# Third cross attention: keys split into F32R parts and replaced in place; both 16-head attentions: exponentials ahead of the chunk copies

## The reference, cut to what matters

```python
q = (x @ Wq).reshape(b, n, h, d).transpose(0, 2, 1, 3)
k = (context @ Wk).reshape(b, -1, h, d).transpose(0, 2, 1, 3)
v = (context @ Wv).reshape(b, -1, h, d).transpose(0, 2, 1, 3)
sim = jnp.einsum('bhid,bhjd->bhij', q, k) * d ** -0.5
attn = jax.nn.softmax(sim, axis=-1)
out = jnp.einsum('bhij,bhjd->bhid', attn, v)
return out.transpose(0, 2, 1, 3).reshape(b, n, h * d) @ Wo + bo
```

## Time and profile before

| | before |
|---|---|
| median of the runs | 2400.94 us |
| profiled execution, own time | 2401.57 us |
| its span | 2399.7 us |
| PE busy | 2227.5 us (93%) |
| DVE busy | 1857.3 us (77%) |
| ACT busy | 1493.9 us (62%) |
| POOL busy | 686.7 us (29%) |

### The profile page before, as it was taken

The page is one execution under the profiler, slowest core; times in us unless marked ns, Lnnn a source line. Parts: engine busy times, 40 slices in busy tenths (PEclk is TensorE's granted clock), DMA queues, the critical chain, the costliest instruction groups (busy, mean ns, idle before and its releaser), DMA issues.

```text
span 2399.7 us, 49297 instructions
## 1 busy us (share of the span) xinstructions
PE 2227.5 (93%) x14668; PEld 1913.3 (80%) x14669; DVE 1857.3 (77%) x4483; ACT 1493.9 (62%) x3090; POOL 686.7 (29%) x926
## 2 busy tenths in 40 slices
PE   7899999999899999995479999999998999989999
PEld 6788888888698788873257888888886788879998
DVE  3798888888876788887975887887888666866666
ACT  5566666666444677767886666666664655636666
POOL 2255555555412122210001111111102442422334
PEclk9999999999899999997589999999998999989999
DMA  8444454445201444430025445444442000114545
GB/s 216 118 141 129 142 146 142 131 138 147 69 0 37 125 132 126 138 111 16 0 67 152 135 134 152 138 145 140 140 132 62 1 1 2 38 54 141 140 140 158
DMA packets 461646, 256.58 MB, mean 107 GB/s; under 512 B 25664, under 2 KB 442332, under 8 KB 461532
## 3 DMA queue, kind: packets, MB, share of 16 engines
q1 hardware_dynamic: 461532, 255.27, 37.8%
HBM read 150.10 MB, written 105.12 MB: 106 GB/s over the span
## 4 chain that ended last, share of the span: by engine, by line
PE 75%; DVE 11%; ACT 6%; issue 5%; POOL 0%; ACTq 0%; DVEq 0%; POOLq 0%
PE ps_o L904 13%; PE ps_s L891 11%; PE ps_p L87 7%; PE ps_p L89 6%; PE ps_p L88 6%; PE ps_t L881 6%; PE ps_o L1474 3%; PE ps_t L1474 2%; PE ps_t L3129 2%; PE ps_s L3111 2%; PE ps_o L3129 2%; PE ps_s L87 2%; ACT a_keys L1022 2%; DVE a_sm L1197 2%; PE ps_s L89 2%
## 5 line engine op out<-in xcount | busy, mean ns | idle before, releaser
L904 PEld LDWEIGHTS ps_o<-a_val,a_pt 128*128 128x128 f32 (+2 forms) x3200 | 416.3, 193 | 34.9 <-issue 8.4
L904 PE MATMUL ps_o<-a_val,a_pt 128*128 128x128 f32 (+2 forms) x3200 | 426.6, 277 | 5.7 <-ACT a_pt L1059 3.6
L891 PE MATMUL ps_s<-a_keys,a_zt 128*128 128x308 f32 (+1 forms) x1024 | 414.3, 491 | 14.6 <-ACT a_keys L1022 9.8
L1031 ACT ACTIVATE a_stage<-ps_p 128x512 f32<-128x512 f32 (+1 forms) x370 | 221.2, 598 | 277.0 <-PE ps_p L89 275.5
L1197 DVE TENSOR_REDUCE a_sm<-a_e 128x16 f32<-128x1232 f32 (+1 forms) x192 | 234.3, 1220 | 179.4 <-ACT a_e L1067 178.9
L1059 ACT ACTIVATE a_pt<-ps_t 128x512 f32<-128x512 f32 (+1 forms) x448 | 225.1, 505 | 144.0 <-PE ps_t L881 142.7
L1022 ACT ACTIVATE a_keys<-ps_p 128x308 f32<-128x308 f32 x603 | 256.8, 427 | 79.5 <-PE ps_p L89 79.0
L87 PE MATMUL ps_p<-ct_hi,a_mt_hi 96*128 (+1 forms) x603 | 292.2, 485 | 0.0
L881 PE MATMUL ps_t<-ident,a_e 128*128 128x128 f32 (+1 forms) x1600 | 261.8, 276 | 25.1 <-POOL a_e L1214 13.6
L1067 ACT ACTIVATE a_e<-a_e 128x1232 f32<-128x1232 f32 (+1 forms) x192 | 203.9, 1062 | 52.8 <-DVE a_e L1189 36.4
L1214 POOL TENSOR_TENSOR a_e<-a_e,a_rs 128x539 f32<-128x539 f32 (+1 forms) x192 | 165.8, 891 | 231.3 <-DVE a_rs L1202 230.0
(11 more groups left out here) (437 smaller groups left out, 4939.4 us busy)
## 6 DMA issues: line engine op xcount, KB each, us to landing
a_vals<-a_stage SPq DMA_DIRECT2D x160, 512.0 KB, 3.5
a_val<-a_vals SPq DMA_DIRECT2D x128, 576.0 KB
f_w<-in_L_ffn_W_dram SPq DMA_DIRECT2D x129, 256.0 KB, 2.6
a_vals<-a_stage SPq DMA_DIRECT2D x40, 416.0 KB
a_val<-a_vals SPq DMA_DIRECT2D x64, 256.0 KB
a_val<-a_vals SPq DMA_DIRECT2D x128, 40.0 KB
x<-in_x_dram SPq DMA_DIRECT2D x8, 512.0 KB, 7.0
out_dram<-x SPq DMA_DIRECT2D x7, 512.0 KB, 6.7
```

Of the source, the lines that this page charges most:

```text
L891: eng.matmul(c.ps_s[:, b, 0:nh * KEYS], zt, keys[:, h0:h0 + nh, :], start=True, stop=True)\
L904: mm = eng.matmul(c.ps_o[:, (i % 2) * P:(i % 2 + 1) * P], self.pt[0:r, n, :], self.val[0:r, i % 2, n, :], start=(n == 0), stop=(n == self. ...
L1031: eng.activation(self.stage[0:n, slot, BANK * (v % 2):BANK * (v % 2) + BANK], bank[0:n, :], ACT.Copy)\
```

## The change

In the third attention (`split`, and with 16 heads `in_place`) keys and z are kept as a high and a low F32R part, and a score bank is three F32R passes. The key parts have one buffer; the units of the next group are projected after the tile's last score bank, into the places of the heads that this tile's scores have used last. ScalarE copies a projected key unit to a ring of four plain buffers (`keep_keys`), GpSimd casts it to the high part and subtracts for the low part (`split_keys`); for the first group ScalarE writes the high part and DVE the low part. TensorE waits for `key_split` and `zt_split` ahead of a group's first scores. Values are projected in the gaps of the chunks and after the first bank; the value plan changes to three a tile. Staging has two buffers after the first window (which borrows `e` and `pt`). For all attentions the exponentials of t + 1 stand ahead of the chunk copies, except in tile 0. The kernel's other parts are as they were.

```diff
+    RING = 4
...
-        self.rounds = self.units // self.STAGES
+        self.split, self.in_place = split, split and H == 16
+        self.slots = 2 if self.in_place else self.STAGES
+        self.first_rounds = self.units // self.STAGES
+        self.rounds = self.units // self.slots
         self.key_plan = (4, 3, 2, 5, 4, 5, 2, 7) if H == 16 else (2, 2, 1, 2, 2, 2, 2, 3)
         self.val_plan = (3, 4, 4, 2, 3, 2, 2, 0) if H == 16 else (2, 1, 2, 1, 2, 2, 0, 0)
+        self.ahead = self.in_place
+        if self.in_place:
+            self.val_plan = (3, 3, 3, 3, 3, 3, 2, 0)
         self.plan = self.make_plan()
         self.tail = self.make_plan(last=True)
-        self.first = self.vuses + H + self.key_plan[-1]
+        self.early_keys = 2 * self.quads if self.in_place else 0
+        self.lead = self.vuses + H + (0 if self.in_place else 2 * self.quads if self.ahead else self.key_plan[-1])
+        self.first = self.lead + self.early_keys
...
-        self.keys = sb(ctx, n("keys"), [P, 2, GT, H, KEYS], F32)
+        if split:
+            self.keys_hi, self.keys_lo = (sb(ctx, n("keys" + h), [P, 1 if self.in_place else 2, GT * H, KEYS], F32R)
+                                          for h in ("hi", "lo"))
+            self.zt_lo = sb(ctx, n("ztlo"), [P, 2, GT * P], F32R)
+            self.unsplit = sb(ctx, n("unsplit"), [P, self.RING, GT, KEYS], F32)
+        else:
+            self.keys = sb(ctx, n("keys"), [P, 2, GT, H, KEYS], F32)
...
+    def freed_by(self, k, par):
+
+        q = self.quads
+        if self.in_place and par == 0:
+            return [2 * k, 2 * k + 1, 2 * k + 8, 2 * k + 9]
+        return [q * k + j for j in range(q)]
+
+    def make_plan_ahead(self, last):
+
+        plan, place, v = [], 0, 0
+        for i in range(self.WIN):
+            keys = [("k", h) for h in self.freed_by((i + 2) % GT, self.key_group(i) % 2) if not last or i < 2]
+            values = [] if last else [("v", v + n) for n in range(self.val_plan[i])]
+            v += len(values)
+            units = values + keys if self.in_place else keys + values
+            plan.append([(kind, n, place + m) for m, (kind, n) in enumerate(units)])
+            place += len(units)
+        return plan
+
...
-    def scores(self, eng, t, b, zt, keys, first=False):
+    def scores(self, eng, t, b, par, k, first=False):
 
         c = self.core
         h0, nh = self.head_span(b)
         if not first:
             eng.wait_ge(self.scores_read.sem, self.scores_read.at(self.NB * (t - 1) + b + 1))
-        eng.matmul(c.ps_s[:, b, 0:nh * KEYS], zt, keys[:, h0:h0 + nh, :], start=True, stop=True)\
-           .then_inc(self.scores_ready.sem, 1)
+        o, cols = c.ps_s[:, b, 0:nh * KEYS], slice(k * P, k * P + P)
+        if self.split:
+            mm = three_passes(eng, o, [z[:, par, cols] for z in (self.zt_hi, self.zt_lo)],
+                              [self.batch_of(keys, par, k, b) for keys in (self.keys_hi, self.keys_lo)])
+        else:
+            mm = eng.matmul(o, self.zt[:, par, cols], self.keys[:, par, k, h0:h0 + nh, :], start=True, stop=True)
+        mm.then_inc(self.scores_ready.sem, 1)
...
+                if self.split and u - 5 >= self.vuses:
+                    eng.wait_ge(self.key_split.sem, self.key_split.at(u - 5 - self.vuses + 1))
...
+        if self.split:
+            eng.wait_ge(self.zt_split.sem, self.zt_split.at(1))
+            eng.wait_ge(self.key_split.sem, self.key_split.at(self.lead - self.vuses))
         for k in range(2):
             for b in range(self.NB):
-                self.scores(eng, k, b, self.zt[:, 0, k * P:(k + 1) * P], self.keys[:, 0, k], first=k == 0)
+                self.scores(eng, k, b, 0, k, first=k == 0)
+        for n in range(self.early_keys):
+            u = self.lead + n
+            if n >= 2:
+                eng.wait_ge(self.proj_copied.sem, self.proj_copied.at(u - 1))
+            self.project_keys(eng, c.ps_p[:, n % 2, :], 1, self.freed_by(n // self.quads, 1)[n % self.quads])
 
...
+                plan = iter([what for what in self.plan_of(i, last) if not self.in_place or what[0] == "v"])
+                keys = iter([what for what in self.plan_of(i, last) if self.in_place and what[0] == "k"])
+
+                def project_next(n=1, scored=False):
+                    for what in islice(keys if self.in_place and scored else plan, n):
                         self.project(eng, w, i, what, last)
 
                 first_z = self.setup and ends and k == GT - 1
...
+                    if self.split and k == 2 and j == 1 and not ends:
+                        eng.wait_ge(self.zt_split.sem, self.zt_split.at(2 * w + par + 2))
...
+                        if k == 2 and self.split:
+                            eng.wait_ge(self.key_split.sem,
+                                        self.key_split.at(self.keys_for(w, par, b, last) + 1))
+                        elif k == 2:
                             eng.wait_ge(self.proj_copied.sem,
                                         self.proj_copied.at(self.keys_use(w, par, b, last) + 1))
-                        self.scores(eng, t + 2, b, self.zt[:, par2, n2 * P:(n2 + 1) * P], self.keys[:, par2, n2])
-                        project_next()
+                        self.scores(eng, t + 2, b, par2, n2)
+                        project_next(scored=b == self.NB - 1)
                 if k == 1 and not ends:
                     u = self.z_use(w, par)
                     self.turn_z(eng, 2 * w + par + 1, u, self.z_use(0, par) % 2)
...
-                    project_next(self.WIN if j == self.uses - 1 else 1)
+                    project_next(self.WIN if j == self.uses - 1 else 1, scored=True)
...
+    def keep_keys(self, eng, u, bank, n, slot):
+
+        eng.wait_ge(self.key_split.sem, self.key_split.at(n - self.RING + 1))
+        eng.wait_ge(self.proj_done.sem, self.proj_done.at(u + 1))
+        eng.activation(self.unsplit[:, slot, :, :], bank[:, 0:GCOLS].rearrange("p (b k) -> p b k", b=GT), ACT.Copy)\
+           .then_inc(self.proj_copied.sem, 1)
+
...
+        for n in range(self.early_keys):
+            self.keep_keys(eng, self.lead + n, c.ps_p[:, n % 2, :], self.heads + n, (self.heads + n) % self.RING)
+        if self.in_place:
+            eng.wait_ge(self.stored[4].sem, self.stored[4].at(16 * self.first_rounds))
...
-                if more and H == 8:
+                plan = self.plan_of(i, last)
+                before = iter([what for what in plan if not self.in_place or what[0] == "v"])
+                scored = iter([what for what in plan if self.in_place and what[0] == "k"])
+
+                def copy_next(n, keys=0):
+                    for what in islice(before, n):
+                        self.copy_proj(eng, w, i, what, last)
+                    for what in islice(scored, keys):
+                        self.copy_proj(eng, w, i, what, last)
+
+                early = not (isinstance(w, int) and t == 0)
+                if more and early:
                     self.exponentials(eng, t + 1, (k + 1) % 2)
...
                     self.copy_chunks(eng, j, self.pt, self.t_use(w, i, j, last), self.t_slot(i, j, last))
                     if j < self.uses - 1:
                         copy_next(1)
-                if more and H > 8:
+                if more and not early:
                     self.exponentials(eng, t + 1, (k + 1) % 2)
-                copy_next(self.NB)
+                copy_next(self.NB, 1)
                 if k == 1 and not ends:
                     self.copy_zt(eng, 1 - par, self.z_use(w, par), self.z_use(0, par) % 2)
-                copy_next(self.WIN)
+                copy_next(self.WIN, self.WIN)
...
-        first = 0
-        if self.left:
-            window(0, False)
-            first = 1
-        with eng.Fori(first, self.WINDOWS - 1) as w:
+        window(0, False)
+        with eng.Fori(1, self.WINDOWS - 1) as w:
             window(w, False)
         window(self.WINDOWS - 1, True)
...
+    def split_first_keys(self, eng):
+
+        for u in range(self.vuses, self.lead):
+            g, h = (u - self.vuses) // self.heads, (u - self.vuses) % self.heads
+            eng.wait_ge(self.proj_copied.sem, self.proj_copied.at(u + 1))
+            bank = self.core.bank(u % 5)[:, 0:GCOLS].rearrange("p (b k) -> p b k", b=GT)
+            eng.tensor_tensor(self.unit_of(self.keys_lo, g % 2, h), bank,
+                              self.unit_of(self.keys_hi, g % 2, h).bitcast(F32), ALU.subtract)\
+               .then_inc(self.key_split.sem, 1)
+
+    def split_zt(self, eng, g, par, u, slot):
+
+        eng.wait_ge(self.t_copied.sem, self.t_copied.at(u + 1))
+        eng.tensor_tensor(self.zt_lo[:, par, :], self.core.ps_t[:, slot, :],
+                          self.zt_hi[:, par, :].bitcast(F32), ALU.subtract).then_inc(self.zt_split.sem, 1)
 
     def fold_vector(self, eng):
...
+        if self.split:
+            self.split_first_keys(eng)
+            self.split_zt(eng, 0, 0, 0, 0)
         if self.left:
```

(49 more changed lines are left out.)

123 lines of the change are left out of this document (95 added, 28 removed).

## The result

The changed kernel takes 2437.4 us (median; before in the same job 2400.3): 1.0137 times the time of before, 95% interval 1.0120 to 1.0153. Slower, by 29 to 37 us; the forecast was 2462 and its range 2392 to 2495. One of its four executions took 4381.65 us and is no part of ratio and interval, which are of the other three (2433.9 to 2438.2); the quotient of the two medians is 1.0155. The profiled execution took 2436.58 us with a span of 2434.8, 35.1 more than before. TensorE is busy 2221.3 us (91%), DVE 1903.5 (78%), ScalarE 1493.5 (61%), GpSimd 998.7 (41%, from 29%).

What follows compares the result with a forecast made beforehand. TensorE's queue was taken to bound both 16-head attentions. First attention 31, third 9, last groups 20, start of the third 1 and second attention 1 sum to +62 us: 2462 as a median, range 2392 to 2495.

Steps and rivals of the forecast that it cites:

- TensorE bounds both attentions: Both 16-head attentions: TensorE's queue is the bound, with windows of 73.02 us in the first and 71.62 in the third.
- Score products: Third attention: three F32R passes cost 1.66 us a tile instead of 2.08, a gain of 0.42.
- Exponentials first, first attention: First attention: third use of ps_t comes late, stall 0.56 us in five tiles; +4.4 a window, +31 us in all.
- Third attention: Third attention's windows: 68.3 + 3.8 + 0.9 = 73.0 us against 71.6; +9 us over seven windows.
- the stalls of the third use: Third attention: TensorE waits for the third use of ps_t behind the early exponential, 3.8 us a window.
- the seven of 0.30: Third attention: seven tiles of a window each stall 0.30 us at the third use of ps_t.
- the contention: Third attention, i = 0: GpSimd's work slows DVE's normalisation and reaches TensorE, 0.9 us a window.
- What I priced at nothing: Key and z splits on DVE, waits on stored values and the reordered plan: no cost while covered.
- Last groups: Tiles 58 to 61, both 16-head attentions: late scores, 3.5 (3.7) us from shift to reduction instead of 1.3; +20 us.
- Start of the third attention: Prologue of the third attention: cheaper keys, but eight early keys pass through the ring; +1 us in all.
- GpSimd: Third attention: casting and subtracting takes 1.5 us a key; GpSimd some 75 to 87% busy and keeps up.
- rival 1: Both 16-head attentions: stalls do not come, earlier exponential helps DVE and products pay; -33 us, 2368; chance 17%.

Runs made afterwards that it cites:

- x10: x4 with two score passes instead of three in the third attention (low z by high keys left out): 2378.2 us, 0.9896 of before.
- x2: Changed kernel with the exponentials behind the chunk copies again in the first attention alone: 2411.3 us, 1.0032 of before.
- x3: Kernel before with the exponentials ahead of the chunk copies in all attentions except in tile 0, keys unsplit F32: 2452.4 us, 1.0212 of before.
- x4: Changed kernel with the exponential between first and second chunk copy in both 16-head attentions: 2389.9 us, 0.9948 of before.
- x7: Changed kernel with GpSimd's subtraction cut to a quarter (part of the computation left out): 2434.8 us, 1.0129 of before.
- x9: Changed kernel with exponentials last in both 16-head attentions and DVE's z subtraction between maxima and shifts: 2402.4 us, 0.9995 of before.
- x8: Changed kernel with exponentials last in both 16-head attentions and GpSimd's subtraction cut to a quarter: 2408.1 us, 1.0018 of before.
- x6: Changed kernel without the early maximum (mask) in tiles 58 to 61 of both 16-head attentions: 2417.3 us, 1.0056 of before.

## Why the prediction was right, and where not

- **TensorE bounds both attentions:** right for seven of eight tiles of the third (x10). In the first no run took matmuls away; what is shown there is that delays of TensorE lengthened the window (x2, x3).
- **Score products:** 0.42 a tile was forecast. In x4 the third use and the scores, without the projections between, take 1.96 us (1462.90 to 1465.98 less 0.69 and 0.43), before 2.31: 0.35. Passes are 0.21 apart as forecast, but the first one behind an F32 matmul holds 0.30.
- **Exponentials first, first attention:** mechanism right, shown by x2 and x3. The term was too large: 4.4 a window against 2.7, since ScalarE's 0.02 + 1.24 + 0.03 + 0.60 + 0.05 behind the projection copy are in truth 1.13 + 0.64 from start to start, and the exponential starts 0.25 us into the tile and not at 0.38. By tile the windows grew by 0.34 to 0.36 us in i = 2, 4, 5 and 6, of which 0.28 is the late third use and the rest, right behind it, is not explained; by 0.98 in i = 7, 0.25 in i = 0, 0.09 in i = 1, where the third use was late before (1.97), and nothing in i = 3. Seven windows: +19.3 in place of +31.
- **Third attention:** forecast +1.3 a window, measured -0.77. Mis-sized were the stalls of the third use (3.8; in truth 1.0, all in i = 7, which is most of what x4 wins; the seven of 0.30 did not come) and the contention (0.9; x7 says 0.1, and that GpSimd's subtraction is also behind the 0.23 us by which the gaps of i = 0 are late). The products gave 8 x 0.35 = 2.8 and not 3.4. What I priced at nothing, "the key and z splits on DVE", costs 2.1 a window for z alone unless the exponential is early (x9), and the casts waiting behind the keys 1.3 (x8). I compared the order first with the order of before, not with the order last under the new work; the price of an edit depended on its companion.
- **Last groups:** +20 forecast, +17.9 to tile 62 and 2.1 behind it, with the interval from shift to reduction at 3.55 for 3.5. x6 places 10.9 in the early maximum; the rest is the longer loop (7.46 a tile against 6.91 in the third), and the lower clock, which is not in the prediction, has a part that these runs do not separate. So the sum of 20 is met, but in part by luck.
- **Start of the third attention:** +1 forecast, +3.9 measured in its first eight tiles, most of it the clock. Changed kernel and then x6, which does the same work there, each from the first exponential to the second, then to the fourth:

```profile
1302.32:1314.90 12.58, 11.07 (x48) 9.10 (x48) 6.27 (x9) 7.16 (x16) 9.90 (x16) 0.73 0.20 51
1314.90:1334.38 19.48, 17.69 (x112) 16.17 (x112) 16.66 (x27) 9.80 (x20) 13.00 (x19) 0.91 0.38 114
```

```profile
1294.16:1305.08 10.92, 9.19 (x51) 7.41 (x51) 6.29 (x9) 6.77 (x15) 8.38 (x13) 1.00 0.05 11
1305.08:1322.04 16.96, 15.36 (x109) 14.27 (x109) 15.42 (x27) 9.70 (x21) 14.06 (x22) 1.00 0.45 131
```

At 0.73 the first stretch takes 12.58 us, at 1.00 10.92, and the eight tiles take 77.1 in the one, 73.4 in the other (73.2 before). Over the eight tiles the mean clock is 0.94 and 1.00; x2, which does the same work in the same order, takes 73.3 at 1.00, and x7, with less on GpSimd, 74.7 at 0.98. TensorE is idle 1.5 to 1.7 us of the first stretch in both; why the clock fell in one of them only, no run here explains.
- **GpSimd:** 1.27 us a key for 1.5, 73% busy in the window, just under the 75 to 87% that were given.

The 26 us between 62 and 36: 12 in the first attention's windows, 14 in the third's, the rest small and of both signs. The steps that were too large, the overlap of ScalarE's instructions and the stalls of 0.30 in the third attention, erred the same way. In the third attention rival 1 held in part: the earlier exponential delays TensorE in one tile of eight only, and DVE's low part of z comes in time.

## What to carry to other kernels

Ahead of a copy that frees a bank, a long instruction cost here what it made the next use of that bank late. Behind the first such copy it cost nothing in the third attention, where it still started 1.5 us earlier than in the kernel before (1.13 against 2.62 us into the tile), and 0.1 us a tile in the first, where another copy stood behind it. Look for that middle place before choosing between first and last. When an edit moves work onto another engine, price every order of the old work again beside it, and a shortcut such as an early maximum again when its input comes later.

## What was not expected of the hardware

Two ScalarE instructions in a row overlap by about 0.1 us in the rows (copy 0.60, next start 0.49 later), enough to halve a stall of 0.56.

DVE and GpSimd stretch each other in other places than forecast. Groups of one window of the third attention, in the windows of the earlier trace rows and above (count, busy us, mean ns, idle before). L236, which writes the layer-normalised z, in the kernel before:

```profile
L236 DVE TENSOR_SCALAR z<-x,ln_mean_var,ln_rstd 128x128 f32<-128x128 f32 x8 | 2.2, 335 | 0.0
```

The product L1352 and L236 in the changed kernel:

```profile
L1352 DVE TENSOR_TENSOR a_e<-a_e,a_rs 128x1232 f32<-128x1232 f32 x8 | 11.9, 1490 | 0.3
L236 DVE TENSOR_SCALAR z<-x,ln_mean_var,ln_rstd 128x128 f32<-128x128 f32 x8 | 4.8, 663 | 0.0
```

L236 takes twice as long with key work beside it, and 428 ns in x7, where three quarters of GpSimd's subtraction are left out. The product L1352 takes hardly more (1442 ns before), and the maxima and shifts from PSUM nothing (576 and 577 ns, before 574 and 575). Where L1352 meets a key, both are longer:

```profile
1461.40 1.83 DVE L1352 TENSOR_TENSOR a_e<-a_e,a_rs 128x1232 f32<-128x1232 f32 x1
1461.87 1.66 POOL L1565 CAST a_keyshi<-a_unsplit 128x308 fp32r<-128x308 f32 x1
```

That is 1.66 us for a cast whose median is 0.44, and 1.83 for a product of 1.44. The Trainium skill, GPSIMD Engine Reference, section Specifications, says that the two share SBUF interfaces and that DVE contends in a two-port mode or with two SBUF inputs. The PSUM rows agree with it; which of its two cases L236 is, no run here shows.
